# Second attention of a two-layer kernel: max-row product over 64 rows, both PV halves and the sums ahead of score round 1

## The reference, cut to what matters

```python
q = jnp.einsum('ntc,hdc->nhtd', x, w_q)          # 16 heads of 64
k = jnp.einsum('ntc,hdc->nhtd', x, w_k)
v = jnp.einsum('ntc,hdc->nhtd', x, w_v)
a = jnp.einsum('nhtd,nhsd->nhts', q, k) / jnp.sqrt(jnp.asarray(dk, x.dtype))
a = jnp.where(mask[None, None], jnp.asarray(-jnp.inf, a.dtype), a)   # causal
a = jax.nn.softmax(a, axis=-1)
y = jnp.einsum('nhts,nhsd->nthd', a, v)
return y.reshape(y.shape[0], y.shape[1], -1) @ w_o
```

## Time and profile before

| what | value |
|---|---|
| median of 3 runs | 3709.71 us (3709.67 to 3718.72) |
| the profiled execution: its time, and its span | 3708.24 us, 3706.5 us |
| PE busy in the span | 2958.0 us, 80% |
| DVE, ACT, POOL busy | 2387.9 us, 1445.8 us, 1051.9 us |
| `attention1` in the span | from about 1510 us to 3100 us |
| mean granted TensorE clock | 0.936 |

### The profile page before, as it was taken

The page is one execution under the profiler, slowest core; times in us unless marked ns, Lnnn a source line. Parts: engine busy times, 40 slices in busy tenths (PEclk is TensorE's granted clock), DMA queues, the critical chain, the costliest instruction groups (busy, mean ns, idle before and its releaser), DMA issues. The chain is left out here.

```text
span 3706.5 us, 66950 instructions
## 1 busy us (share of the span) xinstructions
PE 2958.0 (80%) x21313; PEld 1958.6 (53%) x21313; DVE 2387.9 (64%) x6295; ACT 1445.8 (39%) x2367; POOL 1051.9 (28%) x1256
## 2 busy tenths in 40 slices
PE   0015447777777778599999999999999996999999
PEld 0003324444444444355665565665666565888888
DVE  8988766777777777455555555555556564555555
ACT  0014424444444445244444444444444442223232
POOL 0000041212121211245555554554555451000000
PEclk9997659988888999699999999999999998999999
DMA  1000012322232221100111100011111002101010
GB/s 45 0 6 0 2 32 39 47 40 42 40 44 37 44 37 31 35 31 28 32 33 32 33 30 30 30 33 32 33 33 33 27 28 66 34 23 34 23 34 23
DMA packets 146310, 116.16 MB, mean 31 GB/s; under 512 B 35442, under 2 KB 118899, under 8 KB 146164
## 3 DMA queue, kind: packets, MB, share of 16 engines
q1 hardware_dynamic: 146164, 114.25, 13.1%
HBM read 60.96 MB, written 17.32 MB: 21 GB/s over the span
## 5 line engine op out<-in xcount | busy, mean ns | idle before, releaser
L1396 DVE CUSTOM_DVE_ANT_0 a_scored<-a_pMax,a_causal 128x128 bf16<-128x128 f32 (+3 forms) x1024 | 451.2, 487 | 385.5 <-PE a_pMax L1518 382.7
L1313 ACT ACTIVATE a_PT<-a_pST 128x1024 f32<-128x1024 f32 (+1 forms) x384 | 338.6, 882 | 611.2 <-PE a_pST L1508 607.9
L805 DVE TENSOR_REDUCE a_max<-a_pMax 128x2 f32<-128x256 f32 (+3 forms) x512 | 406.9, 822 | 205.6 <-PE a_pMax L941 197.5
L744 ACT ACTIVATE a_PT<-a_pST 128x512 f32<-128x512 f32 x640 | 370.6, 597 | 403.2 <-PE a_pST L481 264.5
L1262 POOL TENSOR_SCALAR_AFFINE_SELECT a_PT<-a_PT 128x256 f32<-128x256 f32 x512 | 242.6, 486 | 739.0 <-ACT a_PT L1313 723.5
L939 PE MATMUL a_pMax<-a_KS,a_QS 96*128 96x128 bf16 (+3 forms) x1024 | 285.6, 331 | 191.6 <-DMA a_QS<-a_mT 123.3
L1526 PE MATMUL a_pO<-a_PT,a_V 128*64 128x512 f32 (+3 forms) x2048 | 336.4, 450 | 0.5 <-POOL a_PT L1262 0.5
L1799 ACT ACTIVATE m_silu<-m_pG 128x512 f32<-128x512 f32 x256 | 153.3, 599 | 409.3 <-PE m_pG L1891 409.3
L952 PE MATMUL a_pST<-a_QS,a_KS 99*128 99x512 bf16 (+3 forms) x1024 | 257.7, 316 | 17.2 <-ACT a_PT L744 14.4
L939 PEld LDWEIGHTS a_pMax<-a_KS,a_QS 96*128 96x128 bf16 x1024 | 107.4, 106 | 297.8 <-issue 187.0
L1899 PEld LDWEIGHTS m_pY<-m_w,m_hT 128*128 128x128 f32 x2048 | 248.0, 191 | 9.9
(11 more groups left out here) (275 smaller groups left out, 6676.2 us busy)
## 6 DMA issues: line engine op xcount, KB each, us to landing
a_rden<-inverse_sums_dram SPq DMA_DIRECT2D x256, 128.0 KB, 2.9
a_QS<-a_parts SPq DMA_DIRECT2D x192, 64.0 KB
a_KS<-a_parts SPq DMA_DIRECT2D x192, 64.0 KB
a_xn_staged<-xn SPq DMA_DIRECT2D x32, 256.0 KB, 2.4
a_max_rows<-a_mT SPq DMA_DIRECT2D x512, 2.0 KB
a_x<-in_L_attn_x SPq DMA_DIRECT2D x16, 256.0 KB, 3.0
x_dram<-a_att SPq DMA_DIRECT2D x16, 256.0 KB, 4.2
xT_dram<-a_xT SPq DMA_DIRECT2D x16, 256.0 KB, 2.8
```

Source lines behind the costliest of these rows:

```text
L744: a.activation(PT[p][:, k], pST[(5 * p + k) % 2][:], ACT.Exp, scale=SCALE).then_inc(exped.sem, 1)
L805: v.tensor_reduce(MX[:, 2 * p:2 * p + 2, j], pMax[j % 2][:, :, 0:(j + 1) * P], AX.X, ALU.max, negate=True).then_inc(maxed.sem, 1)
L1313: a.activation(PT[s.q % 2][:, :, k * TOK:k * TOK + w], pST[:, :, 0:w], ACT.Exp, scale=SCALE).then_inc(exped.sem, 1)
L1396: last = v.tensor_tensor_reduce(scored[:, cc, at:at + w], pMax[:, cc, at:at + w], causal[:, TOK - w:], -1.0, 3e38, ALU.add, ALU.min, MX[pa ...
```

## The change

Three parts, all in `attention1`:

- The max-row product contracts over 64 rows for each head (0 to 63 and 64 to 127) where it had two. `max_rows` and `ones_rows` are 128 partitions high; rows that carry no maximum are zero. The four DMAs of a step write rows 0, 1, 64 and 65.
- All four blocks of PV of step r-1, and in even steps the sums, stand ahead of score round 1. On ScalarE the copies of PV and sums move ahead of the exponential of round 1, on SyncE the DMA of the sums (L1200) ahead of those of the max rows.
- With that, `turn_m` is followed at once by the projection of q.

```diff
-        MQ = [sb(f"max_rows{i}", [64, TOK], F32R) for i in range(2)]
-        onesr = sb("ones_rows", [64, P], F32R)
+        MQ = [sb(f"max_rows{i}", [P, TOK], F32R) for i in range(2)]
+        onesr = sb("ones_rows", [P, P], F32R)
...
-                        sp.dma_start(MQ[i][32 * h + k:32 * h + k + 1, :].bitcast(F32), mT[at:at + TB, :].bitcast(F32)).then_inc(m_put, 16)
+                        sp.dma_start(MQ[i][DH * h + k:DH * h + k + 1, :].bitcast(F32), mT[at:at + TB, :].bitcast(F32)).then_inc(m_put, 16)
...
                     if s.next_x:
                         store_xT(b + 1)
+                    if s.sums:
+                        sums_compact(s.g - 1)
                     if s.turn_m:
                         m_rows(s.r + 1, (q + 1) % 2)
-                    if s.sums:
-                        sums_compact(s.g - 1)
...
                     exp(s, 0)
-                    exp(s, 1)
-                    if s.turn_m:
-                        m_evac(s.r + 1)
                     if not s.start:
                         o_evac(s.r - 1, (q - 1) % PB)
                     if s.sums:
                         den_evac(s.g - 1)
+                    exp(s, 1)
+                    if s.turn_m:
+                        m_evac(s.r + 1)
...
-                        rows = slice(32 * cc, 32 * cc + 2)
+                        rows = slice(DH * cc, DH * cc + DH)
                         mm = pe.matmul(pST[:, cc, at:at + w], onesr[rows, :], MQ[s.q % 2][rows, queries], start=False, stop=(at, kb) == rounds[-1])
...
-                        weigh(before, (0, 1))
+                        weigh(before, range(TB))
+                    if s.sums:
+                        v_in.wait(pe, 2 * s.g + 1)
+                        sums(s.g - 1, 2 * ((q // 2 - 1) % 2))
                     score_round(s, 1)
                     maximum(1)
...
                         turn_m(r + 1)
-                    if not s.start:
-                        weigh(before, (2, 3))
-                    if s.sums:
-                        v_in.wait(pe, 2 * s.g + 1)
-                        sums(s.g - 1, 2 * ((q // 2 - 1) % 2))
```

## The result

The changed kernel takes **3749.4 us** (median of 4 runs, 3745.24 to 3751.95) against 3712.37 us before (4 runs on the same chip): ratio 1.010, 95% interval 1.0086 to 1.0114. It is slower, by more than a measurement's 0.3%. The forecast was 3731 us, its likeliest case's own range 3705 to 3760.

A forecast was written before the change was run, and what follows sets the result against it. TensorE was taken as the bound in `attention1`, with VectorE/GpSimd and SyncE chains just beneath. 3708.2 - 30 (stretches) + 20 (clock falls, q = 5) + 31 (falls ahead of L1518) = 3729, so 3731 us; own range 3705-3760, all cases 3660-3762.

The forecast's parts named there:

- The padding's 1.1 us a step: TensorE in `attention1`: six borders between array shapes vanish per step, saving 0.39, 0.3 and 0.4 us in rounds 0, 1, 2.
- leg A: Odd step's round 0 L1518 to next even step's round 0 L1508: 10.65 us becomes 9.99, set by SyncE's max-row DMAs.
- Leg C: Even step's round 1 L1508 to odd step's held L1518: 8.92 us becomes 7.98, VectorE held by GpSimd, TensorE waiting 2.1.
- Leg B: Even step, L1508 of round 0 to L1508 of round 1: 3.58 us becomes 4.96, as PV and sums move in.
- The price of a fall: Granted TensorE clock dropping to 0.50 after idling ahead of L1518: 1.6 us less 0.33 of slack, 1.3 us each.
- How often the clock falls: Clock drops after 48 new 2.1 us waits ahead of L1518: half assumed, 24 x 1.3 = +31 us (bounds 12 and 62).
- Sixteen batches gain 30 us: Whole `attention1` without clock drops: a batch of steps goes from 95.96 to 94.08 us, 30 us gained over sixteen.
- No fall of the clock: Rival, chance 0.2: no clock drop at 2.1 us waits, only q = 5 pays: 3700 us; 3675 if that pays nothing.
- The port does not hold L1417: Rival, chance 0.15: VectorE's L1417 does not wait for GpSimd, even-to-odd stretch 6.1 us, 3558 us in all.
- TensorE free of waits: Rival, chance 0.04: only TensorE's own work counts, 9.66 + 4.86 + 5.8 = 20.3 us per two steps, about 3510 us.
- GpSimd goes first at each meeting: Rival, chance 0.06: L1262 before L1417 and L1285 before L1404 add 1 us per even-to-odd stretch, about 3795 us.
- The padding saves nothing: Rival, chance 0.05: 64 rows cost more or padding gains nothing, leaving only the reordering, about 3760 us.

The follow-up runs named there:

- padded kernel with L1417 early: Kernel before plus the 64-row padding, old order kept, with VectorE's L1417 moved ahead of the maxima of round 1: 3567.12 us, ratio 0.961.
- the filling: Changed kernel plus matmuls nobody reads, run while TensorE waits ahead of L1518 of odd steps and L1482: 3691.0 us, ratio 0.993.
- the last version: Changed kernel with L1417 ahead of the maxima of round 1 and, on SyncE, max-row DMAs ahead of the inverse sums' wait and broadcast: 3521.34 us, ratio 0.948.
- padding alone: Kernel before with only the max-row product widened to 64 rows, in the old order: 3635.12 us, ratio 0.979.
- sums back: Changed kernel with the sums, their copy and DMA back behind L1540 as before, PV still joined, L1417 not moved: 3640.11 us, ratio 0.980.
- order alone: Changed kernel without the padding, so the reordering with the max-row product over 2 rows: 3792.17 us, ratio 1.022.

## Why the prediction was right, point by point

- **The padding's 1.1 us a step.** Right within 0.1, but not all of it arrives. From before to the padded kernel with L1417 early, in the same order of TensorE, a pair falls by 2.0 us (23.15 to 21.15), where the prediction's deductions make 2.4 with the old wait of L1518. Most of the rest is held back by others: 0.17 at L1518, and leg A stands at 9.98, bound by SyncE.
- **Leg C**, forecast 7.98: 8.08. Each link was there: L1417 held by L1280, L1262 lengthened (1.10), L1404 held by L1284 (0.93), L1518 0.99 behind the end of L1284. The links were shown by making GpSimd's additions small.
- **Leg B**, forecast 4.96: 4.83 where the max rows were there in time, 4.93 where they were not.
- **Leg A**, forecast 9.99 by SyncE: 9.97. The price of 1.10 for the landing, taken from an early step, measured 1.07. But it shows in 9 of 46 pairs only; in the others the clock fell and TensorE was the later one.
- **The price of a fall**, forecast 1.3: 1.37 (a pair of 24.34 against 22.97), and 1.36 by batches. Also as forecast, leg A's slack pays a part of it.
- **How often the clock falls** is the term that failed: "I take half: 24 x 1.3 = +31 us (bounds 12 and 62)". It was 37 of 46, so 37 x 1.37 = 51 us in place of 31. Taking the middle between 3 of 15 and always was a choice without a row behind it. The falls in q = 5 came each time, as forecast, though at 1.4 us each rather than 1.6: 15 of them, less the three of before at 1.64, are +16 us in place of +20.
- **"Sixteen batches gain 30 us"** was a little too much. In the profiled executions, from one first L1501 to the one 15 batches later, it is 1444.1 us before, 1477.0 after and 1421.0 with the filling. Taking the 3 falls from the first and 49 from the second, 29 are left (the filled run, less its 12, is 1409, and 1410 is left of the second); a batch without a fall is 95.95 before and 94.2 after, 1.7 where I had 1.88. The last batch, which I had let gain like the others, lost about 3, perhaps because its last steps have no projections to cover the same chain; no run shows that. So the gain was 26.
- **The balance**: the spans differ by 40.2. Falls are +66 of it (71 in the changed kernel less the 5 of before), which leaves -26 for the legs; the second number is found by taking off the first, so their sum is no test. The forecast had -30 and +51. Both misses have the same sign, and the sum, 18 us low, stayed inside its own range. That the time came out right is owed in part to the width of that range, since how often the clock falls was a guess.
- **`turn_m`'s border** of 0.20: wrong, and free of consequences. L1488 starts 0.03 behind L1540 (2414.06 to 2414.09). Nobody could use the time in leg C, which was held anyway.
- **The rivals.** *No fall of the clock* had 3700, with falls in q = 5 alone, and 3675 with none at all. The run with the wait filled has none, and with its 12 us of filling taken off it is 3679. *The port does not hold L1417* gave 3558 for what measured 3555 once GpSimd was quiet. *TensorE free of waits*, 3510: the last version, in which almost nothing waits, has legs of 9.69, 4.82 and 5.99 against 9.66, 4.86 and 5.8, and takes 3521. *GpSimd goes first at each meeting* did not happen: L1417 ended 1.08 behind L1280, and L1262 was the one drawn out. *The padding saves nothing* fell with the padding alone.

## What to carry to other kernels

Before moving work on the bounding engine, ask where the chains of the other engines start. What stands between a chain's start and its end on that engine is hidden; what is moved ahead of the start is paid, unless the chain itself waited for that engine further on (here the sums were paid in full, and PV hardly at all). When a saving turns into idle time, look for the one instruction of the chain that need not be in it: moving L1417 by two places turned a loss of 1% into a gain of over 4.5%. And try the parts of a change one by one, since here a part worth -76 us and one worth +114 came together.

## What the runs showed of the hardware that I had not expected

- A transpose with 16 columns of weights (L1540) and the full-width product behind it start 0.03 us apart, while the same transpose ahead of PV, with 64 columns, took 0.20. So not every change of a tile's width costs a border.
- L1404 has one input, 8 integers a partition, and is held by L1284 like L1417 is by L1280: 0.93 us, 0.24 with the additions small. VectorE's L1388, with one input in PSUM and one in SBUF, is not: it lasts 0.69 from 2420.64, beside GpSimd's L1285 (2420.56 to 2421.30), and takes no longer than elsewhere (0.69 in the padded kernel's low part of q, with GpSimd idle).
- The granted clock fell more often after short waits than I had thought. Waits, with the mean idle time by the brackets and how many were followed by a fall:

| wait | kernel | us | falls |
|---|---|---|---|
| L1518 | padding alone | 0.9 | 0 of 46 |
| L1518 | sums back | 1.0 | 0 of 46 |
| L1482 | padding, L1417 early | 1.1 | 0 of 15 |
| L1518 | order alone | 1.4 | 17 of 46 |
| L1482 | before | 1.6 | 3 of 15 |
| L1518 | after | 1.9 | 37 of 46 |
| L1482 | padding alone | 2.0 | 13 of 15 |
| L1482 | sums back | 2.1 | 12 of 15 |
| L1482 | order alone | 2.8 | 10 of 15 |
| L1482 | after | 3.1 | 15 of 15 |

The length of the wait alone doesn't decide, and what else does these runs don't tell.
